# Value products of two blocks in one burst in every second slot, in place of one block's in every slot

## The reference

```python
q = (x @ Wq + bq)...; k = (x @ Wk + bk)...; v = (x @ Wv + bv)...      # 16 heads of 32
scores = einsum('bhqd,bhkd->bhqk', q / sqrt(32), k) + attention_bias
scores = where(src_mask, -inf, scores)
probs = softmax(scores)
ctx = einsum('bhqk,bhkd->bhqd', probs, v)
x = x + (ctx @ Wo + bo)
```

## Time and profile before

| | |
|---|---|
| median of 3 runs | 2577.67 us (2573.52 to 2578.06) |
| the profiled execution | 2573.42 us, its span 2571.6 us |
| mean granted clock of TensorE | 0.973 of full speed |
| busy: PE, PEld | 2424.2 us (94%), 1909.9 us (74%) |
| busy: DVE, ACT, POOL | 1342.5, 990.1, 982.8 us |
| the attention stage in the trace | about 892 to 1797 us |

### The profile page before, as it was taken

The page is one execution under the profiler, slowest core; times in us unless marked ns, Lnnn a source line. Parts: engine busy times, 40 slices in busy tenths (PEclk is TensorE's granted clock), DMA queues, the critical chain, the costliest instruction groups (busy, mean ns, idle before and its releaser), DMA issues. The chain is left out here.

```text
span 2571.6 us, 44303 instructions
## 1 busy us (share of the span) xinstructions
PE 2424.2 (94%) x16100; PEld 1909.9 (74%) x16100; DVE 1342.5 (52%) x2700; ACT 990.1 (38%) x1977; POOL 982.8 (38%) x806
## 2 busy tenths in 40 slices
PE   5999999999998499999999999998589999999999
PEld 4687787777776367777777777776478888888887
DVE  5354454444444577777677667776433323333322
ACT  3231331331331376766666666666212111211211
POOL 0031431422422367767676667765022012102200
PEclk9999999999999699999999999999789999999999
DMA  5201101101101565555556555553411101110100
GB/s 166 75 17 58 41 16 57 41 16 57 41 1 41 188 185 177 178 190 162 180 166 200 162 173 177 174 171 126 153 56 50 49 0 49 49 49 0 49 33 17
DMA packets 133361, 243.69 MB, mean 95 GB/s; under 512 B 13212, under 2 KB 17452, under 8 KB 133184
## 3 DMA queue, kind: packets, MB, share of 16 engines
q1 hardware_dynamic: 133184, 241.39, 29.1%
HBM read 216.17 MB, written 25.20 MB: 94 GB/s over the span
## 5 line engine op out<-in xcount | busy, mean ns | idle before, releaser
L951 POOL TENSOR_TENSOR at_bias<-at_bias,at_mask 128x512 f32<-128x512 f32 x512 | 590.3, 1179 | 309.5 <-DMA at_bias<-in_fside_Bx16xSxS 270.8
L487 ACT ACTIVATE L_hid<-L_turn,L_b1c 128x512 f32<-128x512 f32 x256 | 176.2, 689 | 982.8 <-PE L_turn L285 977.7
L648 DVE CAST L_hh<-L_hid 128x512 fp32r<-128x512 f32 x256 | 123.6, 483 | 795.5 <-PE L_acc L746 756.8
L283 PE MATMUL L_turn<-L_xth,L_w1h 128*128 128x512 f32 x1024 | 406.5, 397 | 7.7 <-ACT L_hid L487 5.4
L744 PE MATMUL L_acc<-L_w2h,L_hh 128*128 128x512 f32 x1024 | 403.3, 394 | 7.6 <-DVE L_hl L650 7.6
L284 PE MATMUL L_turn<-L_xth,L_w1l 128*128 128x512 f32 x1024 | 400.6, 391 | 0.0
L746 PE MATMUL L_acc<-L_w2l,L_hh 128*128 128x512 f32 x1024 | 400.4, 391 | 0.0
L745 PE MATMUL L_acc<-L_w2h,L_hl 128*128 128x512 f32 x1024 | 400.3, 391 | 0.0
L285 PE MATMUL L_turn<-L_xtl,L_w1h 128*128 128x512 f32 x1024 | 400.0, 391 | 0.0
L982 ACT ACTIVATE at_bias<-at_bias,at_neg_top 128x512 f32<-128x512 f32 x512 | 362.9, 713 | 1.3 <-DVE at_neg_top L1105 1.3
L1105 DVE CUSTOM_DVE_ANT_0 at_bias<-at_score,at_bias 128x512 f32<-128x512 f32 x512 | 332.7, 684 | 50.1 <-PE at_score L1259 25.9
(11 more groups left out here) (206 smaller groups left out, 3036.1 us busy)
## 6 DMA issues: line engine op xcount, KB each, us to landing
at_bias<-in_fside_Bx16xSxS SPq DMA_DIRECT2D x256, 512.0 KB, 3.7
L_xin<-in_x SPq DMA_DIRECT2D x8, 1024.0 KB, 5.4
L_xres<-in_x SPq DMA_DIRECT2D x8, 1024.0 KB, 5.5
at_xin<-x_scratch SPq DMA_DIRECT2D x8, 1024.0 KB, 5.9
at_xres<-x_scratch SPq DMA_DIRECT2D x8, 1024.0 KB, 6.3
L_xin<-x_scratch SPq DMA_DIRECT2D x8, 1024.0 KB, 5.6
L_xres<-x_scratch SPq DMA_DIRECT2D x8, 1024.0 KB, 5.5
x_scratch<-L_xres SPq DMA_DIRECT2D x7, 1024.0 KB, 4.3
```

The lines of the kernel that those rows point to most:

```text
L283: nc_mm = pe.matmul(out, ah, bh, start=i == 0, stop=False)
L951: nc.gpsimd.tensor_tensor(tile, tile, mask[:, m % TT, :], ALU.add).then_inc(masked, 1)
```

## The change

In an even slot PE issues the contexts of the two blocks before it, one right behind the other, between the scores and the transposes. In an odd slot it issues none. At slot 0 of a batch the two are blocks 14 and 15 of the batch before; after the last batch the last two are issued together. The order of everything else, the buffers, the waits inside `context` and the programs of the other engines stay.

```diff
                     after = following(b, m, last)
                     if after:
                         scores(*after)
-                    if m:
-                        context(b, odd, m - 1, first)
-                    elif not first:
-                        context(b - 1, 1 - odd, BLOCKS - 1, False)
+                    if m % 2 == 0:
+                        for before in (m - 2, m - 1):
+                            if m:
+                                context(b, odd, before, first)
+                            elif not first:
+                                context(b - 1, 1 - odd, BLOCKS + before, False)
...
             each_pair(pe, body)
-            context(B - 1, (B - 1) % 2, BLOCKS - 1, False)
+            for m in (BLOCKS - 2, BLOCKS - 1):
+                context(B - 1, (B - 1) % 2, m, False)
```

## The result

After: 2592.76 us median of 6 runs (2591.05 to 2596.3), against 2577.86 for before (2573.52 to 2580.76) on the same chip. Ratio 1.0059 (95%: 1.0046 to 1.0072), or +14.9 us: slower, inside the range 2577 to 2598 and 4.8 us above the forecast of 2588. The profiled execution took 2596.3 (span 2594.5), 22.9 more than that of before; the two lie at opposite ends of what their kernels scatter over. Both differences are needed: slots are compared in the profiles, kernels by their medians.

The account below looks back on a forecast made before the run. PE was taken to bound the attention stage. Terms 8.6, 3.6 (slots 7, 11), -2.9 (slots 3, 13, 15), 1.4, -1.0 and 0.9 gave +10.6 us, which on the median 2577.67 made 2588; range 2577 to 2598.

Parts of the forecast that it names:

- Second context in the burst 0.87: Even slots: a context right behind another adds eight rounds of 0.11, 0.87 us, instead of the full 1.01.
- The rival of the full 1.01: Even slots: the second context costs its full 1.01 us; +8.8 us, 2597, chance 0.1.
- Nothing regained beyond 1.01 in odd slots, pair at -0.14: Odd slots: leaving out the context saves only its own 1.01 us; a pair without a new wait gains 0.14.
- The bank gates the projection at 1.70 and 2.03: Odd slots: projection waits for PSUM bank gen until 1.70 us after slot start (7, 11) or 2.03 (1, 5).
- The first rival: Tiling switch saved and bank gen no bar: each of 63 pairs saves 0.14, 8.8 us faster, 2569, chance 0.1.
- Slots 1 and 5, 8.6: Pairs with odd slots 1 and 5: bank gen leaves late, so 15 pairs cost 0.57 each, +8.6 us.
- The spread, 1.4: Slots 3, 7, 11, 15: DVE's inverse spread delays its at_turn copy; 0.1 for 14 such slots, +1.4 us.
- Slots 8 and 9, -1.0: Slot 8 costs 0.43 in 7 batches, slot 9 gives 4.0 back: -1.0 us together.
- The 4.0 taken back in slot 9: Slot 9, batches 2 to 6: low-clock stretches let the projection start earlier, 4.0 us back in all.
- The rest, 0.9: Slots without projection (1 to 3 of batch 0, 8 to 15 of the last), tail included: +0.9 us.
- the clock stays up: Slots 8 and 9: the burst fills PE's idle time and removes low-clock stretches; +4.8 us, 2582.5, chance 0.2.
- The clock falls more often: Idle in odd slots, or batches 0 and 1 too: four more clock falls at 2.4, +9.6 us, 2598, chance 0.1.

Follow-up runs that it names:

- e4: The changed kernel, all bursts kept, with the second unit's transposes ahead of the projection's first quarter in slots 1, 5, 7, 11: 2580.29 us, 1.0019 of before.
- e2: Before, with two contexts together only in slots 2, 6, 12 and none in slots 1, 5, 11: 2591.48 us, 1.0069 of before.
- e1: Before, with two contexts together only in slots 0, 4, 14 and none in slots 15, 3, 13: 2570.12 us, 0.9975 of before.
- e8: The changed kernel, second unit's transposes ahead in slots 1, 5, 7, 11, DVE's spread after its second-unit copy (slots 3, 7, 11, 15): 2593.46 us, 1.0069 of before.
- e10: Before, with bursts in slots 0, 4, 8, 12, 14; in slot 11 second unit's transposes ahead and spread after the copy: 2565.39 us, 0.9943 of before.
- e3: Before, with two contexts together only in slots 8 and 10 and none in slots 7 and 9: 2577.19 us, 1.0007 of before.
- e9: Before, with two contexts together only in slot 8 and none in slot 7: 2570.82 us, 0.9962 of before.
- e5: Before, with two contexts together only in slots 0, 4, 8, 14 and none in slots 15, 3, 7, 13: 2567.64 us, 0.9961 of before.
- e6: Before, with bursts only in slots 0, 4, 8, 14 and DVE's spread after its second-unit copy in slots 3, 7, 11, 15: 2581.57 us, 1.0019 of before.
- e7: Before, without bursts, only DVE's spread moved after its second-unit copy in slots 3, 7, 11, 15: 2589.92 us, 1.0048 of before.

## Why the prediction was right, step by step

- *Second context in the burst 0.87*: right. Even slots other than slot 8 grew by 0.87 to 0.89, and 1.89 - 1.01 = 0.88. The rival of the full 1.01 falls.
- *Nothing regained beyond 1.01 in odd slots, pair at -0.14*: right in slots 2 and 3 (-0.14) and, without batch 2, in 12 and 13 (-0.13). The Trainium skill, in TensorEngine Tiling (Array Packing), Key Properties, has a change of tiling mode drain the engine. The trace agrees as far as the seam saved is worth 0.14, and by that rule alone the kernel would have become faster; that is what the pairs with nothing else in the way show, and slots 1, 5, 7 and 11 show what it leaves out.
- *The bank gates the projection at 1.70 and 2.03*: right, 1.70 and 2.01. It is the largest term. That it is a cause is shown by e4, where other work under the same wait gave back 6.6 us in slots 1 and 5, and by e2 against e1. The first rival (the bank is no bar) falls.
- *Slots 1 and 5, 8.6*: 15 x 0.61 = 9.2.
- *The spread, 1.4*: too small. Against the gates (-0.63, and -1.01 in slot 15) slot 7 is short by 0.06 in 8 batches, slot 11 by 0.27 in 7 and slot 15 by 0.28 in 7: 4.3. I had bounded it at 0.2 a slot for 14 slots; some lose more than half a microsecond. Slot 15 of batch 2 in after's timeline:

```profile
1232.71 1.38 DVE L1121 COPY at_normal<-at_inv 128x512 f32<-128x512 f32 x1
...
1234.01 0.68 DVE L1112 COPY at_pt<-at_turn 128x512 f32<-128x512 f32 x1
...
1234.84 0.63 PE L1288 MATMUL at_turn<-ident,at_bias 128*128 128x128 f32 x4 [0.26 <-DVE at_pt L1112]
```

The mean of the spread is 0.85, but this one took 1.38: where a copy has to be in time every time, the long ones count. e8 and e10, with the spread behind the copy in slot 11 and the second unit's transposes ahead, got all of it back there; e4, with the transposes alone, did not.
- *Slots 8 and 9, -1.0*: wrong in sign here. Slot 8 at full clock cost about what was said: 15.47 for the two slots in e4's batch 2 against 15.06, +0.41 for +0.43 forecast, which is 2.9 over seven batches. The 4.0 taken back in slot 9 assumed that the low stretches stay where they were. They don't: in after the two slots took 6.7 more in all, in e4 and e8 0.8 more, in e3 4.7 less, with the same order of contexts in both slots. So a forecast of -1.0 can't be confirmed or refuted by one profile. The prediction named a differing clock in these slots as a sign of being wrong, and it differs (0.81 in after's batch 0, where before had full clock): the forecast took the low stretches for part of the program.
- *The rest, 0.9*: 3.7 in this profile, of which 2.8 is the last slot's own fall of the clock, in after's timeline:

```profile
1801.71 1.65 PE L1259 MATMUL at_score<-at_nat 32*128 32x512 f32 x12 [0.41 <-DVE at_neg_top L1105]
...
1803.30 3.64 PE L1276 MATMUL at_ctx<-at_pt,at_v 128*32 128x128 f32 x64
...
1806.87 1.54 PE L1288 MATMUL at_turn<-ident,at_bias 128*128 128x128 f32 x8
```

The burst takes 3.57 there, against 1.89 at full clock; e4 with the same last slot has +0.67 in place of +3.48. Without it, 0.9.

So the profiled difference of 22.9 is 12.5 for the seven kinds of pair beside slots 8 and 9 (10.7 forecast, spread in both; batch 3's -0.87 is in the 12.5), 6.7 for slots 8 and 9 (-1.0), and 3.7 for the rest (0.9). The last two hold the clock, which scatters between executions; the median difference of 14.9 stands for the others. The forecast of +10.6 was 4.3 short of it. The mis-sized terms are the spread (2.9 too small), slots 1 and 5 (0.6) and slot 8 with 9 (3.9 too small without any gain from the clock): together 18.0. The 3 us between that and 14.9 aren't settled. The recorded clocks don't account for them: after's six runs have 0.971 to 0.974, 0.9727 on average, against 0.9735 for the 52 of before, which would add 1.7 us and not take any away. That the total came within 4.8 us of the forecast, with terms 7.4 short, is partly luck.

Of the rivals on the clock, *the clock stays up* falls with the profile (seven batches with a low part in slots 8 and 9, where before had five). *The clock falls more often* was half true of the profiled execution; a difference of 0.0008 between means of runs that scatter by 0.003 and more doesn't show that it holds in the others.

## What to carry to other kernels

When work is pulled out of a slot, it gives back only what the next gate in that slot leaves: find when each resource comes free, counted from the slot's start, and compare it with when the engine would now arrive. A change applied to every slot can be worth keeping in some: here three bursts gained and three others lost more than three times as much, by the medians and by the estimate at equal clock. Before an operation is moved out of one wait's way, list what it will stand in front of. And compare the mean clocks of two kernels before a small gain is put down to an edit.

## What the runs showed of the hardware

TensorE's granted clock differs in the same two slots of the same program. e1 leaves slots 8 and 9 untouched, and its windows for batches 1 and 2 are:

```profile
1057.44:1074.94 17.50, 15.19 (x146) 11.12 (x146) 11.94 (x27) 11.12 (x26) 8.87 (x8) 0.80 0.54 177
1172.12:1188.52 16.40, 13.98 (x147) 10.26 (x146) 11.95 (x27) 11.13 (x26) 9.03 (x8) 0.90 0.60 183
```

Before had batch 1 at 1.00 (15.06) and batch 2 at 0.80 (17.41). Slot 8 holds the longest of the stalls of PE shown above (1.7 us in the waits of after), and a mean of 0.80 or 0.90 is a part at 1.2 GHz and the rest at 2.4. One such difference is worth 1.3 or 2.4 us, as much as nine or seventeen seams saved, so that a single profile can't tell a gain of a few microseconds. The whole runs show the same: over the 52 runs of before the mean clock lay between 0.970 and 0.977 and the time between 2584.2 and 2568.1, the lower clock with the longer time. With the burst in slot 8 and a context left in slot 9 the two slots stayed under 16.8 us in every batch of e9 and e10, against up to 17.5 in before and e1 and 17.9 in after; but in batch 3 of e5, which has the same two slots, they took 18.2. e6, with the same two slots, stayed under 16.9. Over all their runs these four kernels have mean clocks of 0.9762 to 0.9772, 0.0030 to 0.0039 above before on the same chips; but e7, which has no burst at all, has 0.9757, 0.0025 above. That a fuller slot 8 keeps the clock up fits most of this and is not shown.

The same copy of 128 x 512 by DVE (the spread) took from 0.43 to 1.41 us in after, and up to 1.62 in e7. Of the 384 spreads in the twelve traces, 14 ran while POOL ran nothing, and all 14 took 0.43; every longer one lay at least in part beside an addition of POOL. But 41 that lay beside POOL took less than 0.45 too, so what decides is not shown.
